# Causal attention over 16 narrow heads: scores in two orientations, on halves and strips of the array

## The reference

```python
q_lat = (x @ Wq_down).reshape(b, t, H, L)          # H = 16, L = 64; k_lat, v_lat alike
q_c, q_e = q_lat @ Wq_up_c, q_lat @ Wq_up_e        # 4 + 4 dimensions a head
q = concat(q_c, rope(q_e)); k = concat(k_c, rope(k_e)); v = v_lat @ Wv_up
scores = where(causal, (q @ k.T) / sqrt(8), -inf)  # per batch and head, 512 x 512
att = softmax(scores, -1)
y = (att @ v).transpose(0, 2, 1, 3).reshape(b, t, 128)
x = x + y @ Wc                                     # then six layers of windowed attention and FFN
```

## Time and profile before

| | us |
|---|---|
| median of 3 runs | 4156.12 (4153.95 to 4156.75) |
| the profiled execution's own time | 4155.47 |
| its span | 4153.7 |
| mean granted PE clock | 0.971 |
| PE busy | 3814.5 (92%) |
| DVE busy | 3258.6 (78%) |
| ACT busy | 3109.2 (75%) |
| POOL busy | 2498.3 (60%) |

### The profile page before, as it was taken

How to read it: one execution, slowest core, us unless ns; L and a number is a source line. 1 busy time by engine, 2 the same in 40 slices (tenths; PEclk the granted TensorE clock), 3 DMA queues, 4 the chain that set the end, 5 groups by cost and what they waited for, 6 DMA issues and landing times.

```text
span 4153.7 us, 101302 instructions
## 1 busy us (share of the span) xinstructions
PE 3814.5 (92%) x30950; PEld 2939.8 (71%) x31328; DVE 3258.6 (78%) x5635; ACT 3109.2 (75%) x7150; POOL 2498.3 (60%) x2247
## 2 busy tenths in 40 slices
PE   6999998899998999988999989999889999899998
PEld 4666665677766777766777667777667776677776
DVE  5877876888867888768888678887688886788876
ACT  4777776788866888857888668887578886688875
POOL 1221221777745777737777457776377774577763
PEclk9999999999998999998999989999989999999999
DMA  2111111000010000010000100000100000000002
GB/s 79 42 32 31 29 39 35 2 0 0 0 28 1 1 0 0 1 28 1 0 0 0 28 1 1 0 0 1 28 1 0 0 0 28 1 1 0 0 1 68
DMA packets 53261, 52.86 MB, mean 13 GB/s; under 512 B 13574, under 2 KB 40452, under 8 KB 51972
## 3 DMA queue, kind: packets, MB, share of 16 engines
q1 hardware_dynamic: 52996, 49.77, 4.5%
HBM read 28.77 MB, written 4.19 MB: 8 GB/s over the span
## 4 chain that ended last, share of the span: by engine, by line
issue 26%; PE 24%; ACT 24%; DVE 21%; ACTq 2%; DVEq 2%; POOL 1%; SPq 0%; DMA 0%; POOLq 0%
PE bank L357 19%; ACT sb_area L668 12%; DVE sb_ssq L1105 10%; DVE sb_smax L1116 6%; ACT sb_area L777 5%; PE bank L416 3%; ACT sb_lnb L786 3%; ACT sb_lnb L789 3%; DVE sb_area L1093 1%; PE bank L503 1%; POOL sb_area L1336 1%; DVE sb_nmx L1013 1%; DVE sb_area L1119 0%; PE bank L532 0%; DVE sb_area L1009 0%
## 5 line engine op out<-in xcount | busy, mean ns | idle before, releaser
L668 ACT ACTIVATE sb_area<-bank 128x512 f32<-128x512 f32 (+4 forms) x3029 | 1570.3, 553 | 259.0 <-PE bank L357 182.3
L357 PE MATMUL bank<-sb_area 128*64 128x64 f32 (+4 forms) x16624 | 1286.1, 274 | 94.9 <-issue 57.8
L1093 DVE TENSOR_TENSOR sb_area<-bank,sb_rots 128x1024 f32<-128x1024 f32 x768 | 939.2, 1224 | 395.2 <-ACT sb_area L777 394.4
L1311 POOL TENSOR_TENSOR sb_area<-sb_area,sb_rn 128x512 f32<-128x512 f32 x768 | 784.8, 1043 | 608.5 <-ACT sb_rn L793 608.5
L1297 POOL TENSOR_TENSOR sb_area<-sb_area 128x512 f32<-128x512 f32 x768 | 967.9, 1278 | 78.3 <-DVE sb_area L1093 76.2
L357 PEld LDWEIGHTS bank<-sb_area 128*64 128x64 f32 (+2 forms) x16624 | 849.5, 151 | 200.6 <-issue 139.1
L357 PE MATMUL bank<-sb_wqk_hi,sb_xwin 128*128 128x512 f32 x1536 | 729.7, 477 | 53.9 <-DVE sb_xwin L1073 43.6
L357 PE MATMUL bank<-sb_area,sb_wvo 128*128 128x256 f32 x3072 | 728.3, 381 | 3.1 <-DVE sb_xT L1151 3.1
L357 PEld LDWEIGHTS bank<-sb_area,sb_wvo 128*128 128x128 f32 x3072 | 555.0, 190 | 78.3 <-issue 12.8
L503 PE MATMUL bank<-sb_ident,sb_area 128*128 128x128 f32 x3072 | 494.9, 285 | 33.4 <-ACT sb_area L668 31.0
L503 PEld LDWEIGHTS bank<-sb_ident,sb_area 128*128 128x128 f32 x3072 | 358.8, 144 | 227.6 <-issue 160.0
(11 more groups left out here) (103 smaller groups left out, 4861.7 us busy)
## 6 DMA issues: line engine op xcount, KB each, us to landing
sb_xwin<-sb_p SPq DMA_DIRECT2D x256, 64.0 KB, 2.0
sb_area<-in_Wqkv SPq DMA_DIRECT2D x7, 1024.0 KB, 5.8
sb_area<-in_WvT SPq DMA_DIRECT2D x7, 512.0 KB, 7.3
sb_wo_bd<-in_Wo SPq DMA_DIRECT2D x14, 256.0 KB, 8.2
sb_area<-in_x SPq DMA_DIRECT2D x4, 512.0 KB, 5.7
sb_area<-in_x SPq DMA_DIRECT2D x8, 256.0 KB, 2.9
x_plus_causal<-sb_area SPq DMA_DIRECT2D x8, 256.0 KB, 2.3
out<-sb_area SPq DMA_DIRECT2D x8, 256.0 KB, 3.5
```

Source lines behind the costliest of these rows:

```text
L357: return nc.tensor.matmul(o, a, b, start=start, stop=stop, skip_group_check=True)
L668: return nc.scalar.activation(o, i, ACT.Copy)
L1093: tt_(t12[:, c % 2, :, :].rearrange("p u (h d) -> p u h d", h=8), src, bc(rots[:, tt, s, :, :], [P, 2, 8, D], 2), ALU.mult).then_inc(S["ro ...
L1311: pt_(qn[:, c, :].rearrange("p (h d) -> p h d", h=8), qsum[:, c % 2, :].rearrange("p (h d) -> p h d", h=8), r, ALU.mult).then_inc(S["qn"], 1)
```

## The change

- A step now stands for four heads of one batch (a group), and there are 32; all is unrolled, in 45 steps with the lead-in and the way out. Step s does the row scores of group s, turns and stores the maxima of group s-1, and does the column scores, exponentials and weighings of group s-2.
- The stacks are made through DRAM: six stores of 256 KB a batch (`split_out`), then one load of 256 KB for the queries and one for the keys per group (`stack`). Rows are now ordered so that 64 partitions hold two heads of 32 rows each; POOL masks one head of either half (x = 0 or 1), so one buffer serves heads (x, lower half) and (x, upper half).
- Row scores: for each x and query block, two fp32r matmuls on 64-row halves of the array, one head each, into banks 0 and 1, and the mask as four bf16 matmuls on halves (a mask product over 128 rows has to be made twice on 64). DVE reduces both banks in one instruction. Nothing else is done with these scores.
- The 16 maxima columns are turned on PE, split in two parts (ACT and DVE), stored in DRAM and loaded as rows into the masked queries, where the keys' stack holds ones, so that the column scores come out less the maximum.
- Column scores: rows are keys of tile kt, columns the queries from kt*128 on, again as pairs on 64-row halves (banks 2 to 5, two pairs in turn). ACT takes the exponential; it lies as the weighing needs it.
- Weighing: for a key tile four fp32 matmuls with 32 value columns each, one per head, on the four 32-column strips of the array, into 32 partitions each of bank 6. The 32 columns hold values and ones, so that a strip gets the weighed values and the sums of two groups of heads.
- After two groups: copy of bank 6 (`yraw`), a permutation on PE brings the sums beside the values, ACT forms exp(-ln(sum)), DVE multiplies; the output projection has two terms.
- Bank 7 is shared in a fixed order (`m_at`) by projections, values, turned maxima, moved sums and output. The copy of a batch's tokens (`xb`, L970) goes: projections read `xT`.
- SP stores the last batch's sum before it asks for the first layer's weights; ACT waits for the last weighing before it splits them.

In the diff below, the scores and the weighing are PE's, then PE's list for one step, ACT's exponentials, DVE's maxima and SP's transfers of the maxima. In PE's list the two places left out hold, for s % 4 of 0, 1, 2, 3: values, output, projection, projection; and moved sums, projection, moved sums, projection.

```diff
-            def causal_slot(n, b, part):
-                ...
-                    mm(o[:, 0:(qt + 1) * P], qm[:, h % 2, qt, :], stacks[:, 1, h // 4, 0:(qt + 1) * P], True, False)
-                    mm(o[:, qt * P:(qt + 1) * P], identb[:, :], tri[:, :], False, True).then_inc(S["c_score"], 1)
...
+            def rows_of_scores(n, u):
+                hg, x, qt = n % 4, u // 4, u % 4
+                need(pe, "c_max", 8 * n + u)
...
+                for g, rows in ((0, low), (1, high)):
+                    mm(ps[g][:, 0:keys], qm[rows, n % 4, x, queries], stack_k[rows, hg, 0:keys], True, False)
+                for g, rows in ((0, low), (1, high)):
+                    mm(ps[g][:, queries], identb[rows, :], tri[rows, :], False, False)
+                for g, rows in ((0, low), (1, high)):
+                    mm(ps[g][:, queries], identb2[rows, :], tri2[rows, :], False, True).then_inc(S["c_s1"], 1)
+
+            def columns_of_scores(n, p):
+                hg, T_, x = n % 4, p // 2, p % 2
+                need(pe, "c_exp", 12 * n + 2 * p - 2)
+                if p == 0:
+                    pe.wait_ge(S[f"mrow{hg}"], 2 * 16 * (n // 4 + 1))
+                b0 = ps[2 + 2 * p % 4], ps[3 + 2 * p % 4]
...
+                blocks = (((0, 0),), ((1, 0),), ((2, 0), (3, 2 * P)))[T_]
+                for kt, c0 in blocks:
+                    for g, rows in ((0, low), (1, high)):
+                        mm(b0[g][:, c0:c0 + T - kt * P], stack_k[rows, hg, kt * P:(kt + 1) * P], qm[rows, n % 4, x, kt * P:T], c0 == 0, False)
...
+            def weigh_causal(n, kt):
+                a, hg = n // 4, n % 4
+                pe.wait_ge(S["c_exp"], 12 * n + (4, 8, 12, 12)[kt])
...
+                for r in range(4):
+                    m = mm(ps[6][32 * r:32 * r + 32, kt * P:T], v32[:, a % 2, (kt * 4 + r) * 2 + hg // 2, hg % 2, :],
+                           e[:, r, c0:c0 + T - kt * P], hg % 2 == 0 and kt == 0, hg % 2 == 1 and kt == 3)
+                    if kt != 2:
                         m.then_inc(S["c_pv"], 1)
...
+                pair(0)
+                if slot(n1 - 1):
+                    turn_max(n1 - 1)
+                unit(0)
+                weigh(n2 - 1, 2)
+                weigh(n2 - 1, 3)
+                pair(1)
+                unit(1)
...
+                pair(2)
+                unit(2)
+                weigh(n2, 0)
+                unit(3)
+                pair(3)
...
+                unit(4)
+                pair(4)
+                unit(5)
+                weigh(n2, 1)
+                pair(5)
+                unit(6)
+                unit(7)
...
+            def exp_pair(n, p):
...
+                need(act, "c_pv", 12 * (n - 1) + 4 * T_ + 4)
+                for g in range(2):
+                    act.wait_ge(S["c_s2"], 12 * n + 2 * p + g + 1)
+                    nc.scalar.activation((et0, et1, et2)[T_][:, 2 * g + x, :], ps[2 + (2 * p + g) % 4][:, 0:w], ACT.Exp)                        .then_inc(S["c_exp"], 1)
...
+            def maxima(n, u):
+                x, qt = u // 4, u % 4
+                dve.wait_ge(S["c_s1"], 16 * n + 2 * u + 2)
...
+                nc.vector.tensor_reduce(nmx[:, n % 2, 0:16].rearrange("p (g x t) -> p g x t", g=2, t=TT)[:, :, x, qt],
+                                        banks[:, 0:2, 0:(qt + 1) * P], AX.X, ALU.max, negate=True).then_inc(S["c_max"], 1)
...
+            def max_rows(n):
+                sp.wait_ge(S["m_free"], m_at["max", n] + 1)
+                sp.dma_start(mx_rows[n % 2].rearrange("e q t -> q e t"), mrows[0:16, n % 2, :, :].bitcast(F32)).then_inc(S["mx_out"], 16)
+                sp.wait_ge(S["mx_out"], 16 * (n + 1))
+                for part in range(2):
+                    sp.dma_start(qm[3 + 4 * part:P:64, n % 4, :, :].rearrange("p x t -> p (x t)").bitcast(F32),
+                                 mx_rows[n % 2, part].rearrange("(g q) t -> g (q t)", g=2)).then_inc(S[f"mrow{n % 4}"], 16)
```

More of the change, by code:

```diff
@@ L165, in build @@
         at[0] = 0
-        v16 = take(TT, HEADS * (P + DA))
-        ptA = take(4, TT, T)
-        ea_ = take(2, (TT + 1) * TT // 2 * P)
+        et0, et1, et2 = take(4, T), take(4, T - P), take(4, T - P)
+        v32 = take(2, TT * 4 * 2, 2, 32)
         crot = take(4, T)
         ra, rb_ = take(T), take(T)
-        yT = take(T)
+        ysum, yraw, yT = take(T), take(T), take(2, T)
         xb = take(T)
@@ L248, in behind, with valid, slot @@
             return s % TT, i + s // TT
[L252 to L268, removed]
+        SLOTS = B * 4
+        FIRST, LAST = -7, 4 * (B - 1) + 9
+        def valid(a):
+            return 0 <= a < B
+        def slot(n):
+            return 0 <= n < SLOTS
+        m_at = {}
+        for s in range(FIRST, LAST + 1):
+            for name, there in ((("max", s - 1), slot(s - 1)),
+                                ((("v", s // 4), ("out", (s - 9) // 4), ("rope", (s + 6) // 4, 1), ("rope", (s + 5) // 4, 2))[s % 4],
+                                 valid((s // 4, (s - 9) // 4, (s + 6) // 4, (s + 5) // 4)[s % 4])),
+                                ((("perm", (s - 4) // 4, 0), ("rope", (s + 7) // 4, 0), ("perm", (s - 6) // 4, 1),
+                                  ("rope", (s + 5) // 4, 3))[s % 4],
+                                 valid(((s - 4) // 4, (s + 7) // 4, (s - 6) // 4, (s + 5) // 4)[s % 4]))):
+                if there:
+                    m_at[name] = len(m_at)
         def need(eng, name, v):
@@ L290, in _ @@
             sp.dma_start(crot, ins["c_crot"]).then_inc(S["c_weights"], 16)
[L292 to L313, removed]
+            sp.dma_start(xres[:, 0, :, :], xd[0]).then_inc(S["res_in"], 16)
@@ new lines, in move_sums, with causal_out @@
+            def move_sums(a, j):
+                o = bank_m("perm", a, j)
+                pe.wait_ge(S["c_yraw"], 2 * a + j + 1)
+                mm(o, perm, yraw).then_inc(S["c_perm"], 1)
+            def causal_out(a):
+                o = bank_m("out", a)
+                pe.wait_ge(S["yT_ready"], 2 * a + 2)
+                for t in range(TT):
+                    mm(o[:, t * P:(t + 1) * P], yT[:, 0, t * P:(t + 1) * P], wc[:, 0, :], True, False)
+                    m = mm(o[:, t * P:(t + 1) * P], yT[:, 1, t * P:(t + 1) * P], wc[:, 1, :], False, True)
+                m.then_inc(S["ca_mm"], 1)
```

413 lines of the change are left out of this document (260 added, 153 removed).

## The result

The changed kernel takes 4022.78 us (median of 4 runs, 4019.53 to 4032.09) against 4156.43 (4153.95 to 4157.64): ratio 0.9683, 95% interval 0.9666 to 0.9700, so 3.2% faster. The forecast was 4011, range 3900 to 4105. The profiled execution took 4023.40 us, its span 4021.5.

The account below looks back on a forecast made before the run. PE's fp32 streams and transposes were taken to bound the old stage; the new step was ring 14.0 plus losses 1.0. 4155.5 + 32 x 15.0 + 17.5 - 649.2 - 1 + 8 = 4010.8 us (4011), range 3900 to 4105.

Parts of the forecast that it names:

- The stage is PE's fp32 streams and transposes: Old causal stage: PE's fp32 streams and transposes set it, at 20.3 us for four heads.
- Pairs and strips stream together: PE's tiled matmuls: paired row halves priced as one, four column strips as fully together; wholly serial strips +6.5 us a step.
- the forecast's units: PE's eight row-score units in a step, widths 1 to 4 blocks twice: 0.28 to 0.44 us each, 2.86 for eight.
- a step near 15.5: Step length estimated from the skill page's 2.38x for three column strips, between strips by two (17.2) and the forecast (15.0).
- The ring: Single row-score banks: PE's next unit waits for DVE's reduction; each gap is the longer of that and PE's list; step 14.0 us.
- U0, U1, U3, U5: Row-score units, numbered 0 to 7 within a step; gaps behind these four filled by PE's list: 1.40, mean 1.82, 1.60, 1.50 us.
- The gap behind U7: After a step's last row-score unit, PE waits for DVE's reduction: 1.49 us, then the next step's first column scores and turned maxima.
- Losses of 1.0 us a step: Added to the 14.0 us step for holes in PE, after the old stage's 12% to seams and clock; bounds 0 and 2.
- half clock for half the stage: Rival: PE at half clock for about half the stage, 22.6 us a step there, S = 18.3, 4116 us; chance 0.08.
- a granted clock under 0.9 from 60 to 560 us: Listed sign that the forecast is wrong: low granted clock over that stretch.
- SP and the maxima hidden: Maxima's round trip through DRAM, 8.2 us, wanted a step (14) later; some 11 us of SP in the fullest step, hidden.
- Front, drain, tail: Around the 32 steps: front net -1 us, drain 17.5, tail to layer 0's weights +8.

Follow-up runs that it names:

- the one-strip kernel: Changed kernel with all four heads of a weighing sent to the same 32-column strip instead of four, output left wrong: 4213.06 us (1 run).
- one line moved: Changed kernel with the weighing of key tile 1 moved from the gap behind row-score unit 5 to behind unit 6: 3993.37 us.
- the turn moved too: The kernel with one line moved, with the turn of the maxima also put behind the weighings of tiles 2 and 3 that follow row-score unit 0: 3986.98 us.
- half reductions: Changed kernel with each row-score reduction reading only the first half of its keys: 3952.21 us.
- the ring open and the order spread: Kernel with two pairs of row-score banks (3987.65), pair products spread between row scores and the turn put behind the weighings of tiles 2 and 3: 3929.36 us.
- double reductions: Changed kernel with each row-score reduction done twice, into two columns of the maxima: 4216.45 us (1 run).
- two pairs of banks and the old order: Changed kernel with row scores alternating between two pairs of banks and column scores on one pair instead of two: 3987.65 us.

## Why the prediction was right

*The stage is PE's fp32 streams and transposes.* With the 1280 transposes gone and the products paired, PE's busy time in the stage fell from 601 to 402 us (387.28 + 15.15).

*Pairs and strips stream together.* Pairs of row halves: the forecast's units add up in the table above. Strips: shown by the one-strip kernel, 2.55 us on eight records. The eight records of tile 1 (three blocks wide, row 559.80) take 0.85 us; less a way out of 0.2 that is the forecast's 0.65. The forecast had no row for this and chose between ends 6.5 us a step apart. It chose right, by analogy: that is luck in part.

*The Trainium skill, "TensorE: Matmul & The Clock Gate", Measured speedup vs the span model*, gives 2.38x for three strips; the forecast's estimate from it was a step near 15.5. This case's four strips of fp32 save 2.55 of the 2.6 us that a full quarter would, and the measurement decides.

*The ring.* 14.13 as the mean of full-clock steps against 14.0 (13.85 and 0.15 for DVE), and right for its reason: halving what DVE does in the gaps is worth 1.44 us a full-clock step with single banks and 0.42 with double ones. Two parts were off and made up for each other in part. Gaps filled by PE's own list were cheaper than priced, by 0.06 to 0.12 us each (U0, U1, U3, U5; U1 against 1.93). The gap behind U7 was 0.61 too short in the forecast, because the turn was left out of the series (0.20 from its start to U0's) and DVE's rotation in front of the last reduction counted at 0.15 for the whole step (it starts about 0.3 late). PE waits for DVE behind U2, U3, U4, U6 and U7; "U3, U6 and U7" was named.

*Losses of 1.0 us a step.* 0.9 was measured, but the kind was left open; the full-clock steps of 14.1 say that it is nearly all clock. That the size came so near is luck: 1.0 was the middle of its bounds, and moving one line left 0.27. Small changes moved the clock from 105 us on: 0.92 to 0.98 with one line moved, 0.99 with the turn moved too, 0.98 with half reductions, 1.00 with the ring open and the order spread, 0.78 with double reductions. The rival "half clock for half the stage" had the right mechanism; 48% of the stage at the low level came to pass in the kernel with double reductions, against 21% in this one. Its 22.6 us for a step at the low level was summed too low: with every PE term doubled, the changes of array mode too, the forecast's list gives 24.9, and the rival's time about 4150. By the forecast's own sign of being wrong (a granted clock under 0.9 from 60 to 560 us) this kernel stands at the edge, with 0.896 once the first 40 us count at the low level. The Trainium skill, "TensorE: Matmul & The Clock Gate", "A second HAM failure mode: psum-queue depth-cycling", says that small gaps between groups over cycled banks make the clock oscillate; the trace agrees in that both levels occur in the stage, and it puts the low one at 14% of the time from 102 us on (a mean of 0.93) and the 40 us before that, by the mask pairs.

*SP and the maxima hidden.* The turned maxima leave at 415.25, the replicated rows are asked for at 418.25 and are used a step later; no wait of PE in the stretch has a DMA as its releaser. Right.

*Front, drain, tail.* The first score came at 62.09 and not 59.7 (60.7 less 1; +2.4): 8 projections on one bank alternate with DVE's rotations at the low clock, 2.07 us each. The 32 steps took 481.7 for 480 (+1.7), part of it because batch 1's rotations stand in DVE's queue ahead of the first reduction (62.08 to 65.41). The drain took 19.3 for 17.5 (+1.8). The weights were asked for 9.2 us after the last weighing for 8 (+1.2) and used 10.8 later for 9.5 (+1.3). With the 4.2 lost in the layers that is 12.6 us: the whole of 4023.4 less 4010.8. So the distance to the forecast is not in the step, which carries the result, but in the seams, each of which was priced a little too low.

*What stays open.* Which pattern of gaps lets the clock fall: from 105 us on it is 0.99 in the kernel with the turn moved (a step of 13.90) and 0.94 in the one with two pairs of banks and the old order, which does PE's same work in 13.57 and so waits less. The sum of the waits alone does not tell. The 4.2 us in the layers were not followed up. Whether the first reduction could be had 3.3 us earlier was not tried.

## What to carry to other kernels

When two engines hand one set of banks to and fro, price each gap as the longer of the producer's own list and the consumer's time plus both ways, in the order in which they are issued; then fill the gaps where the consumer is longer, and only then buy banks. Opening such a ring brought 35 us here with the old order and 93 with the order spread, which gives room to the engine that lost its banks as well. Test a suspected bound by making it shorter as well as longer, and read what it is worth from steps that stand wholly at full clock: both changes moved the granted clock (0.92 to 0.98 and to 0.78), and the median holds both effects in one number.

## What the runs showed of the hardware

- Four matmuls on 128x32 strips of columns, fp32 with two records each, stream fully together: eight records of 512 columns take 2.55 us longer when they share a strip (3.77 against 1.22).
- The clock column can print 1.00 over matmuls at the low level: for 62 to 102 us it does, while mask pairs take 0.33 us instead of 0.23. In another kernel the same stretch, with the same 0.33, prints 0.50.
- A 512-column cast on DVE took 1.20 us (425.38) beside POOL's two products (424.25) and 0.43 with POOL idle (49.55); the reduction at 424.50, which reads a bank, kept its 0.96 beside the same two products. In the grouped instructions, with both kinds of cast together, it is

```profile
L1121 DVE CAST sb_p<-sb_area 128x512 fp32r<-128x512 f32 x13 | 10.7, 826 | 0.1
```

- A turn of the maxima on a strip between two groups of row halves puts off the second group by 0.20 us from start to start, the change of array mode back to halves included (the change towards it falls into PE's wait). Moved behind the W' strips it saves 0.30 us there and costs 0.22 in its new gap. The forecast charged 0.2 for each change alone.
